# Spreading the scan's tokens over the state rows: four matmuls on 32 rows for two steps, in place of two on all rows for each step

## What is computed

```python
x = x + attention(x, q, k, v, w, u weights, cond, heads=16)
# second block, B=8, S=1024, d_inner=1024, d_state=16
xr, gate = split(x @ W_in.T)                 # 2 x 1024 columns
xc = silu(causal_conv4(xr + t_emb) + b)      # 3 taps on VectorE, 1 on ScalarE
xn = layernorm(xc) * ln_g + ln_b
Bm, Cm, dt = split(xn @ W_xproj.T); dt = tanh(dt @ W_dt.T + b_dt) * 0.01
for t in range(1024):
    h = clip(h * ad[t] + bd[t] * xn[t], -10, 10)     # h: (8, 16, 1024)
    y[t] = einsum('bd,bdh->bh', C[t], h)
x = x + ((y + D * xn) * silu(gate)) @ W_out.T
```

## Time and profile before

| what | value |
|---|---|
| median of three runs | 6129.4 us |
| the profiled execution's own time | 6129.35 us |
| its span | 6127.5 us |
| busy over the span | TensorE 5746.3 us (94%), VectorE 4416.0 (72%), GpSimd 3186.1 (52%), ScalarE 2395.1 (39%) |
| granted TensorE clock, mean | 0.969 |
| steps of the scan | 3326 to 6060 us |

### The profile page before, as it was taken

One profiled execution on the slowest core, in us unless ns is written; L12 is line 12 of the kernel. 1 busy time (PEld: TensorE's weight loads), 2 busy tenths in 40 slices (PEclk: granted clock), 3 DMA queues, 4 the chain that ended last, 5 costly groups with the idle time before them and its releaser, 6 DMA issues.

```text
span 6127.5 us, 73179 instructions
## 1 busy us (share of the span) xinstructions
PE 5746.3 (94%) x24000; PEld 2734.0 (45%) x24000; DVE 4416.0 (72%) x5676; ACT 2395.1 (39%) x4692; POOL 3186.1 (52%) x2561
## 2 busy tenths in 40 slices
PE   7999999999999999999986779899999999899998
PEld 3444444444444444444433334444454444444444
DVE  4656556566565665655635999899998989899984
ACT  2444444444444454444444424334252424334111
POOL 1876667767676676766745223424243342424213
PEclk7999999999999999999987989999999999999999
DMA  2332323323233232332224343444444453444433
GB/s 87 85 97 67 102 65 106 92 72 98 73 95 92 74 98 76 90 92 73 74 65 137 83 115 101 139 98 125 120 120 135 113 147 92 131 115 128 122 95 115
DMA packets 411564, 613.29 MB, mean 100 GB/s; under 512 B 58768, under 2 KB 189968, under 8 KB 410672
## 3 DMA queue, kind: packets, MB, share of 16 engines
q1 hardware_dynamic: 374320, 558.24, 32.7%
q10 hardware_dynamic: 36864, 50.38, 3.3%
HBM read 305.31 MB, written 201.38 MB: 83 GB/s over the span
## 4 chain that ended last, share of the span: by engine, by line
PE 68%; DVE 18%; issue 5%; DMA 3%; ACTq 2%; ACT 2%; POOL 1%; SPq 1%; DVEq 1%; POOLq 0%
DVE g L2093 9%; PE bank L787 8%; PE bank L817 8%; PE bank L775 6%; PE misc L804 5%; PE xps L1808 5%; DVE g L2099 4%; PE yps L1822 4%; PE miscb L1832 4%; PE bank L746 3%; PE bank L728 3%; PE miscb L1862 3%; PE bank L756 3%; PE miscb L1765 2%; PE yps L1862 2%
## 5 line engine op out<-in xcount | busy, mean ns | idle before, releaser
L1128 POOL TENSOR_TENSOR acc<-acc,prob 128x512 f32<-128x512 f32 x1536 | 1906.5, 1277 | 837.9 <-PE bank L817 567.6
L1057 DVE TENSOR_REDUCE mx<-bank 128x1 f32<-128x512 f32 x2048 | 1307.0, 684 | 541.2 <-PE bank L787 534.9
L2093 DVE SCALAR_TENSOR_TENSOR g<-xps,bd,g 128x1024 f32<-128x1024 f32 x1024 | 1313.2, 1282 | 171.7 <-PE xps L1808 143.0
L1808 PE MATMUL xps<-sx,spread 128*128 128x512 f32 x2048 | 914.8, 531 | 158.7 <-DVE g L2093 143.7
L950 ACT ACTIVATE prob<-misc 128x512 f32<-128x512 f32 x1277 | 713.3, 599 | 743.5 <-PE misc L804 661.5
L787 PE MATMUL bank<-khat,qhat 96*128 96x512 f32 x2048 | 938.9, 519 | 5.9 <-DVE mx L1057 0.9
L2099 DVE TENSOR_SCALAR g<-g,lim 128x1024 f32<-128x1024 f32 x1024 | 843.0, 823 | 33.7
L1808 PEld LDWEIGHTS xps<-sx,spread 128*128 128x128 f32 x2048 | 362.1, 195 | 660.7 <-issue 354.0
L804 PE MATMUL misc<-qhat,khat 98*128 98x512 f32 x1443 | 602.5, 460 | 17.4 <-ACT prob L950 11.5
L787 PEld LDWEIGHTS bank<-khat,qhat 96*128 96x128 f32 x2048 | 373.3, 191 | 533.6 <-issue 381.4
L1822 PE MATMUL yps<-g,cexp 128*32 128x512 f32 x4096 | 516.9, 623 | 0.0
(11 more groups left out here) (240 smaller groups left out, 7659.0 us busy)
## 6 DMA issues: line engine op xcount, KB each, us to landing
sx<-scratch_xhl SPq DMA_DIRECT2D x512, 128.0 KB, 4.9
scratch_dx<-dx SPq DMA_DIRECT2D x64, 512.0 KB, 2.7
scratch_xhl<-xhi SPq DMA_DIRECT2D x64, 512.0 KB, 4.3
scratch_xhl<-xn SPq DMA_DIRECT2D x64, 512.0 KB, 4.6
scratch_y<-ysb SPq DMA_DIRECT2D x512, 64.0 KB
early<-scratch_dx SPq DMA_DIRECT2D x59, 512.0 KB, 4.5
early<-scratch_y SPq DMA_DIRECT2D x59, 512.0 KB, 4.0
xt_n<-in_x SPq DMA_DIRECT2D x112, 256.0 KB, 3.0
```

What stands on the lines that cost most here:

```text
L1057: dve.tensor_reduce(self.mx2[:, h * TT + qt, c:c + 1], bank[m][:, 0:QC], AX.X, ALU.max).then_inc(sem[f"dve_m{m}"], 1)
L1128: pool.tensor_tensor(self.acc[:, a, h, :], self.acc[:, a, h, :], self.prob[:, (n % 2) * GH + h, :], ALU.add).then_inc(sem["pool_acc"], 1)
L1808: mm = pe.matmul(self.xps[t % 2][:, half * BANK:(half + 1) * BANK], self.spread[:, 2 * part + half, :], self.sx[:, n % 2, wd, :], start=Tr ...
L2093: dve.scalar_tensor_tensor(self.g[:, t % STATES, :], self.xps[t % 2][:, :], self.bd[:, i % 2, tl:tl + 1], self.g[:, (t - 1) % STATES, :], ...
```

## The change

Piece x now exists for even t alone and makes the tokens of steps t and t+1. It issues four matmuls, each over its own block of 32 partitions of `spread` and `sx`, and each into its own PSUM bank: both halves of xps[0] and of xps[1]. So it waits for q(t-1), the last reader of either buffer, where x(t) waited for q(t-2). Both q(t) and q(t+1) wait for x(t). In the load, part 0 now holds the even tokens of the unit and part 1 the odd ones; the load waits for the x of the last pair of the unit before last. In the planner, x has its old duration of 0.45 us, is due at t less 4, and is listed behind q(t-1).

```diff
             put(n * UNIT - 12.0, "SP", 2.2, ("lu", n), (rows if n * UNIT % TOK == 0 else ()) + (
-                (("x", (n - 1) * UNIT - 1),) if n > 1 else (("rest",),)), [(f"ld_sx{n % 2}", 64)], lands=4.0)
+                (("x", (n - 1) * UNIT - 2),) if n > 1 else (("rest",),)), [(f"ld_sx{n % 2}", 64)], lands=4.0)
 
         def x_of(t):
-            put(t - 2.0, "PE", 0.45, ("x", t), (("lu", t // UNIT),) + ((("q", t - 2),) if t > 1 else ()), [("pe_xps", 1)])
+            put(t - 1.0, "PE", 0.45, ("x", t), (("lu", t // UNIT),) + ((("q", t - 1),) if t else ()), [("pe_xps", 1)])
         for n in range(2):
             load(n)
-        x_of(0), x_of(1)
+        x_of(0)
         for t in range(last):
             i, tl = divmod(t, TOK)
-            put(t, "DVE", 1.3, ("q", t), (("x", t),) + ((("g", t - 1),) if t else (("g0",),)) + ((("d3", i),) if tl == 0 else ()) + (
+            put(t, "DVE", 1.3, ("q", t), (("x", t // 2 * 2),) + ((("g", t - 1),) if t else (("g0",),)) + ((("d3", i),) if tl == 0 else ()) + (
                 (("out", (t - STATES) // 4 * 4),) if t >= STATES else ()), [("dve_q", 1)], step=t)
-            if t + 2 < last:
-                x_of(t + 2)
+            if t % 2 and t + 1 < last:
+                x_of(t + 1)
...
             elif kind == "lu":
-                i, s, t0, wd = n * UNIT // TOK, n % 2, n * UNIT, UNIT // 2
+                i, s, t0 = n * UNIT // TOK, n % 2, n * UNIT
...
                 if n > 1:
-                    w.wait_ge(sem["pe_xps"], plan.after("pe_xps", ("x", (n - 1) * UNIT - 1)))
+                    w.wait_ge(sem["pe_xps"], plan.after("pe_xps", ("x", (n - 1) * UNIT - 2)))
...
                     sp.dma_start(self.sx[32 * j:32 * j + 2 * B, s, :, :].bitcast(F32),
-                                 d["xhl"][:, :, t0 + part * wd:t0 + (part + 1) * wd, half * BANK:(half + 1) * BANK].rearrange(
-                                     "h b t c -> (h b) t c").bitcast(F32)).then_inc(sem[f"ld_sx{s}"], 16)
+                                 d["xhl"][:, :, t0:t0 + UNIT, half * BANK:(half + 1) * BANK].rearrange(
+                                     "h b (w u) c -> u (h b) w c", u=2)[part].bitcast(F32)).then_inc(sem[f"ld_sx{s}"], 16)
...
             elif kind == "x":
-                part, wd = divmod(r, UNIT // 2)
...
-                if t > 1:
-                    w.wait_ge(sem["dve_q"], plan.after("dve_q", ("q", t - 2)))
-                for half in range(2):
-
-                    mm = pe.matmul(self.xps[t % 2][:, half * BANK:(half + 1) * BANK], self.spread[:, 2 * part + half, :],
-                                   self.sx[:, n % 2, wd, :], start=True, stop=True)
+                if t:
+                    w.wait_ge(sem["dve_q"], plan.after("dve_q", ("q", t - 1)))
+
+                for j in range(4):
+                    part, half = divmod(j, 2)
+                    of = slice(32 * j, 32 * (j + 1))
+                    mm = pe.matmul(self.xps[part][:, half * BANK:(half + 1) * BANK], self.spread[of, j, :],
+                                   self.sx[of, n % 2, r // 2, :], start=True, stop=True)
                 mm.then_inc(sem["pe_xps"], 1)
...
-                w.wait_ge(sem["pe_xps"], plan.after("pe_xps", ("x", t)))
+                w.wait_ge(sem["pe_xps"], plan.after("pe_xps", ("x", t // 2 * 2)))
```

## The result

The changed kernel takes 6177.9 us (median of four runs, 6158.87 to 6180.67) against 6131.6 before: a ratio of 1.0061, interval 1.0046 to 1.0076, so slower by 37 us by the ratio and 46 by the medians, where 51 us less were forecast. Its profiled execution has a span of 6173.7 us. Up to 3326 us the two traces agree; the steps take 2784 us in place of 2734.

The account below looks back on a forecast made before the run. VectorE and TensorE were both close to full, neither share alone deciding. Removing 143 us of VectorE's waits for x and adding 92 gave -51 us from 6129.35: 6078 us, range 6015 to 6280.

Parts of the forecast that it names:

- the queue moves to VectorE: Rival, between g(t-1) and q(t) of even t: x stays late behind side work, +148 us, 6277 us; chance 0.26.
- array time given back: On TensorE, four x matmuls take 0.49 us with borders instead of 0.92: 0.43 us a pair, 220 us in 512 pairs.
- the half that was named: Sign that the forecast is right: x's busy time on TensorE falls from 914.8 us to near half.
- Lateness: How late x comes on TensorE, behind side work and out; taken as halved because the queue gets shorter.
- the cover: How late x may be without delaying q: 2.14 us before; after, 0.20 without a tap, 0.95 with one.
- the sum of the waits after: VectorE's waits for x after the change: 336 pairs at 0.09 us and 176 at 0.35, 92 us.
- at most 336 have a tap: Of 512 pairs, 336 were counted with a VectorE tap of 0.75 us behind g(t-1), 176 without.
- The prediction's own formula: x's lateness: 37% none, 10% at 3.6 us, 54% even from 0 to 2.14, scaled; what exceeds the cover is waited.
- my reading of rows 7: Going from out to the next product, a tiling border costs only an exposed weight load, 0.13 us, no full drain.
- if lateness stays, +148: With x's lateness as before, VectorE waits 291 us for x against 143 removed: 148 us slower.
- its point of decision: The rival of the queue moving to VectorE decides if lateness stays above about two thirds of the kernel before's.
- The serial rival: x's four matmuls run one after another, nothing is given back: +371 us, 6500 us; chance 0.10.

Follow-up runs that it names:

- e4_split: The kernel before, second buffer kept, with the two x matmuls of a step each over their own 32 rows: 6192.2 us, 1.0119 of the kernel before.
- e11_splittwice: The kernel before with two row-block x matmuls a step, each pair issued twice, 0.23 us of streaming more a step: 6401.3 us, 1.0453 of the kernel before.
- e5_load: The changed kernel with the first matmul of 240 side-product groups issued twice, 206 us of array work more: 6327.2 us, 1.0346 of the kernel before.
- e3_full: The changed kernel with each of x's four matmuls over all 128 rows, one after another: 6315.3 us, 1.0318 of the kernel before.

## Why the prediction was wrong, point by point

**The outcome.** The time of 6178 us lies within the range of 6015 to 6280, but on the other side of the kernel before than the forecast of 6078; slower had 0.36. The sign named for the case that the queue moves to VectorE, a wait above 200 us with the array time given back, is what came: 206.6.

**Right.** The four run side by side, loads included; the busy time of x fell even below the half that was named. The time from x's load to q is 0.63. Lateness was nearly halved: read off the timelines, from q's end to x's load less 0.06 us, it averages 0.64 us over the pairs, and 1.13 over the steps of before, measured from q(t-2) there. With no tap in between, the cover is 0.20. A pair with work to cover the gap waits 0.08 us, where 0.09 was charged.

**The step that failed is the sum of the waits after: 92 us forecast, 206.6 measured.** It was made of 336 pairs with a tap at 0.09 us and 176 without at 0.35. Counted over the timeline of the changed kernel, only 123 of 512 pairs have a tap between q(t-1) and q(t), and 224 have any VectorE work there beside g; these wait 19 us in sum, 0.08 each. The other 287 wait 179 us, 0.62 each, and the first pair 9. So two terms were off. The bare pairs are 287 and not 176: "at most 336 have a tap" was taken as if all had one, while 137 taps stood ahead of an odd q, and some pairs had several. And the wait of a bare pair is 0.62, not 0.35, since lateness isn't even from 0 to 1.07: 66 of these waits are of 0.5 to 1 us, a product of 0.86 us just begun, and some 24 of 2 to 3 us are chains, 15 of them with the clock at its lower level for part of the time. Nor was the tail before what was read from the waits: 182 x were more than 2.14 us late and not 98, and other VectorE work covered the rest. The prediction's own formula, with 224 and 287 pairs and lateness at 0.64/1.13 = 0.57 of before, gives 147 us, which is no gain at all; the rest of the 206.6 is the first pair's 9 us and a tail heavier than the formula's.

**Two smaller terms.** The array time given back was put at 0.43 us a pair. A border costs more than an exposed load: what is given back is 0.29 a pair in a dense stream (0.92 less 0.63), and 0.38 on average by e4_split and e11_splittwice (0.92 less 0.54), if four blocks cost what two do, as they did in the dense stream. Here the rule of the Trainium skill that the prediction weighed (TensorEngine Tiling (Array Packing), Key Properties: changing the tiling mode drains the engine) agrees with the trace better than my reading of rows 7 did: 0.40 us for two borders, between my 0.26 and the 0.6 of two full drains with loads. And "if lateness stays, +148" was low: e5_load, with the array time handed back, stands 212 us over before.

**So the account is**: the loss of the second buffer about 210 us (e5_load), array time given back 0.29 to 0.38 x 512 = 150 to 195 us at 0.85 (e5_load), 127 to 166 us. The difference is 46 to 85 us slower, against 37 measured. This is a way to share out the time and no independent check: 212 and 0.85 both come from e5_load set against the changed kernel, so they must return nearly 37. The second buffer was never taken away by itself, with one x a step behind q(t-1), and the two sums hold the effect of the clock. The rival "the queue moves to VectorE" named the place and the mechanism, and its point of decision (lateness above two thirds of today's) was set too high: the mean did fall, to 0.57, and the kernel was slower all the same.

**The serial rival** was priced at +371 and measured, in e3_full, at +195. The likely reason, not tried by itself: while VectorE waits, TensorE catches up, and lateness falls, where my sum added the longer time to an unchanged lateness.

## What to carry to other kernels

Time on a full engine is worth little if the change that frees it takes a buffer away: price the slack that the buffer gave (here 3.06 - 0.92 = 2.14 us, afterwards 0.20) against the whole distribution of how late the producer is, a product just begun and chains apart, and not its mean. When a producer must answer within a fraction of a us, its in-order queue has to hold itself back for it: the change became a gain of 0.2% over the kernel before once the planner let x go ahead of side work by 0.6 us, and of 0.4% in the best of the orders tried after that. And an island of another tiling mode costs its two borders each time; here it paid in array time for four short matmuls (0.63 us in place of 0.92 to 0.94) and not for two (0.62 in place of 0.46). Last, time freed on TensorE can come back as a lower clock: look at the granted clock of the stretch before and after, and at the spacing of the loads in front of the late instruction.

## What the runs showed of the hardware

Matmuls on four blocks of 32 rows, with 128 columns of weights and 512 moving each, load their weights together in 0.19 us and are done in 0.50, into four PSUM banks. From their load to the next load is 0.43 us, of which the load has 0.19; so, as an estimate, the four stream in 0.24 where four full-row ones take 0.92: 3.8 times. A second pair in e11_splittwice added the same 0.24 (0.86 less 0.62). An island of them in a dense stream costs 0.63 us, 0.40 of it at the two borders, so that 1.5 times is left; an island of two costs the same. The Trainium skill (TensorE: Matmul & The Clock Gate, Measured speedup vs the span model) gives 3.07 for four row tiles; the streaming alone was better here, the island worse. Less TensorE work brought a lower granted clock over the steps, 0.97 to 0.92, and in the first chunk, busy 228 of 330 us where it was 254, 0.89 to 0.78; matmuls put in idle time brought part of it back and won nothing.
